# Opening of a two-layer cross-attention and FFN kernel: transposes, first scores and first maxima in another order

## What is computed

```python
def _L0_xattn_ref(Q, K, V, Wq, bq, Wk, bk, Wv, bv, Wo, bo):
    Qh = _split_heads(Q @ Wq.T + bq)
    Kh = _split_heads(K @ Wk.T + bk)
    Vh = _split_heads(V @ Wv.T + bv)
    scores = jnp.einsum('bhqd,bhkd->bhqk', Qh, Kh) / scale
    scores = scores - jnp.max(scores, axis=-1, keepdims=True)
    attn = jax.nn.softmax(scores, axis=-1)
    attn = jnp.clip(attn, EPS, None)
    attn = attn / jnp.sum(attn, axis=-1, keepdims=True)
    ctx = jnp.einsum('bhqk,bhkd->bhqd', attn, Vh)
    ...
def fp4_quant_dequant(x):
    xb = x.reshape(shape[:-1] + (shape[-1] // BLOCK, BLOCK))
    scale = jnp.max(jnp.abs(xb), axis=-1, keepdims=True) / 6.0
    ...
x = x + _L0_xattn_ref(_layernorm(x, axis=-1), ctx_1024, ctx_1024, ...)
x = x + _L0_ffn_ref(_layernorm(x, axis=-1), L0_ffn_w_gate, L0_ffn_w_up, L0_ffn_w_down)
x = x + _L1_xattn_ref(_layernorm(x, axis=-1), ctx_1024, ctx_1024, mask_BxSxS2_bk1, ...)
x = x + _L1_ffn_ref(_layernorm(x, axis=-1), L1_ffn_w1, L1_ffn_b1, L1_ffn_w2, L1_ffn_b2)
```

## Time and profile before

| | before |
|---|---|
| median of 3 runs | 927.75 us (927.74 to 927.95) |
| profiled execution, its own time | 927.82 us |
| its span, first to last instruction | 926.0 us |
| TensorE, VectorE, ScalarE, GpSimd busy | 97%, 72%, 65%, 22% of the span |
| granted TensorE clock | 1.000 |

### The profile page before, as it was taken

The page is one execution under the profiler, slowest core; times in us unless marked ns, Lnnn a source line. Parts: engine busy times, 40 slices in busy tenths (PEclk is TensorE's granted clock), DMA queues, the critical chain, the costliest instruction groups (busy, mean ns, idle before and its releaser), DMA issues.

```text
span 926.0 us, 16209 instructions
## 1 busy us (share of the span) xinstructions
PE 900.5 (97%) x5610; PEld 601.8 (65%) x5610; DVE 669.8 (72%) x2179; ACT 602.1 (65%) x1671; POOL 204.6 (22%) x316
## 2 busy tenths in 40 slices
PE   6899999999999999999999999999999999999998
PEld 3555576767665567576675566667757655757786
DVE  5999883763989786475598978367478988837568
ACT  3888425972789643795378953499257984269845
POOL 3211001862000000486000000077400000028600
PEclk9999999999999999999999999999999999999999
DMA  9500000000000000000000010000000000000000
GB/s 294 212 1 2 29 1 23 2 1 1 1 1 25 1 28 24 1 1 2 1 0 8 18 29 1 24 1 1 1 0 1 19 7 1 1 0 2 2 1 23
DMA packets 14560, 18.35 MB, mean 20 GB/s; under 512 B 3088, under 2 KB 11664, under 8 KB 14480
## 3 DMA queue, kind: packets, MB, share of 16 engines
q1 hardware_dynamic: 12288, 15.40, 5.0%
q10 hardware_dynamic: 2064, 1.91, 0.7%
q0 software_dynamic: 128, 0.01, 0.0%
HBM read 15.21 MB, written 2.10 MB: 19 GB/s over the span
## 4 chain that ended last, share of the span: by engine, by line
PE 76%; DVE 13%; ACT 8%; issue 3%; DMA 1%; SPq 0%; DVEq 0%; ACTq 0%
PE bank L1243 28%; PE bank L1258 10%; PE bank L1526 6%; PE bank L1624 6%; PE bank L1506 6%; PE bank L1358 5%; PE bank L1414 4%; ACT ring L671 4%; DVE row_max L1050 3%; PE bank L1391 3%; PE bank L1481 1%; PE bank L1492 1%; PE bank L1251 1%; PE bank L1430 1%; ACT ring L715 1%
## 5 line engine op out<-in xcount | busy, mean ns | idle before, releaser
L463 POOL TENSOR_TENSOR rstd<-var_eps,minus_half 128x2 f32<-128x2 f32 x32 | 23.3, 734 | 533.1 <-DVE var_eps L886 533.1
L481 POOL TENSOR_TENSOR ring<-ring,row_inv 128x256 f32<-128x256 f32 x192 | 112.1, 613 | 95.4 <-DVE row_inv L1145 95.4
L556 ACT ACTIVATE ring<-bank 128x512 f32<-128x512 f32 x224 | 123.6, 612 | 14.1 <-PE bank L1258 12.6
L1258 PE MATMUL bank<-ident_s,ring 128*128 128x128 f32 x768 | 105.0, 279 | 5.1 <-DVE ring L1058 2.7
L1258 PEld LDWEIGHTS bank<-ident_s,ring 128*128 128x128 f32 x768 | 82.8, 141 | 39.2 <-issue 15.7
L715 ACT ACTIVATE ring<-ring,row_max 128x256 f32<-128x256 f32 x192 | 95.1, 497 | 17.3 <-DVE row_max L1138 17.3
L671 ACT ACTIVATE ring<-bank,row_max 128x256 f32<-128x256 f32 x192 | 88.4, 496 | 5.7 <-DVE row_max L1050 5.7
L1138 DVE CUSTOM_DVE_ANT_0 ring<-bank,maskbias 128x256 f32<-128x256 f32 x192 | 70.7, 420 | 23.4 <-issue 23.4
L1050 DVE TENSOR_REDUCE row_max<-bank 128x2 f32<-128x512 f32 x128 | 79.4, 684 | 5.9 <-PE bank L1391 5.2
L1243 PE MATMUL bank<-wgu_s,act_s 128*128 128x352 f32 x256 | 78.4, 459 | 0.0
L1243 PE MATMUL bank<-ctxT_s,wk_s 128*128 128x512 f32 x160 | 76.4, 600 | 0.0
(11 more groups left out here) (192 smaller groups left out, 1753.3 us busy)
## 6 DMA issues: line engine op xcount, KB each, us to landing
x_s<-x SPq DMA_DIRECT2D x4, 512.0 KB, 3.9
ctxT_s<-ctxT SPq DMA_DIRECT2D x4, 512.0 KB, 4.2
w_s<-w SPq DMA_DIRECT2D x2, 1024.0 KB, 16.3
out<-act_s SPq DMA_DIRECT2D x16, 128.0 KB, 1.7
wk_s<-wk SPq DMA_DIRECT2D x1, 1024.0 KB, 13.4
wv_s<-wv SPq DMA_DIRECT2D x1, 1024.0 KB, 14.7
wq_s<-wq SPq DMA_DIRECT2D x1, 1024.0 KB, 16.2
wo_s<-wo SPq DMA_DIRECT2D x1, 1024.0 KB, 17.5
```

The lines of the kernel that those rows point to most:

```text
L481: ins = pool.tensor_tensor(probs1[i % PRING1][:, a, :], probs1[i % PRING1][:, a, :], row_inv[:, i, a:a + 1].to_broadcast([P, SEQ]), ALU.mult)
L556: act.activation(probsT[u % TRING][:, :, :].rearrange("p a q -> p (a q)"), psum(at, key)[:], ACT.Copy).then_inc(drain(at, key), 1)
L1258: ins = pe.transpose(psum(at, key)[:, c * SEQ + a * P:c * SEQ + (a + 1) * P], tile[:, a, c * P:(c + 1) * P], ident_s[:])
```

## The change

Five edits, all of the opening; nothing is computed differently.

- TensorE transposes `xn0` first, then makes key chunk 0, then the queries and the scores of round 0, and only then key chunk 1 and the values. The wait for the values' weights moves behind the scores.
- The banks of `xT0`, `k0` and `q0` follow: key chunk 1 goes to bank 7 instead of 1, the queries to banks 5 and 6 instead of 0 and 7.
- ScalarE takes out both halves of `xT0` and key chunk 0 ahead of `piece_steps(0)`; key chunk 1 is taken out between the second and the third unit's exponentials of round 0.
- VectorE takes the four maxima of round 0 ahead of `scale_piece(1)`, which now stands ahead of the values.

```diff
@@ jobs_layer0 @@
     for c in range(KEY_CHUNKS):
-        jobs.add(("k0", c), c)
+        jobs.add(("k0", c), c if with_last_layer else 7 * c)
...
     for c in range(KEY_CHUNKS):
-        jobs.add(("q0", c), c if with_last_layer else 7 * c)
+        jobs.add(("q0", c), c if with_last_layer else 5 + c)
@@ scalar: layer0_heads @@
                         for i in round_units0(r):
+                            if i == 2 and with_weights:
+                                layer0_keys(at, [1])
                             exponentials(i)
@@ scalar: opening @@
             act.wait_ge(keys_loaded, 16 * 4)
+            layer0_inputs(opening_pass)
+            layer0_keys(opening_pass, [0])
 
             piece_steps(0)
-            layer0_keys(opening_pass, [0])
-            layer0_inputs(opening_pass)
-            layer0_keys(opening_pass, [1])
             act.wait_ge(query_mask, 6)
@@ vector: layer0_heads @@
                         if g is None:
+                            scale_piece(1)
                             dve.wait_ge(values_loaded, 16 * 2)
@@ vector: opening @@
             round_piece(0)
-            scale_piece(1)
             dve.wait_ge(consts_set, 6)
@@ tensor: opening @@
-            pe.wait_ge(wk0_packed, 1)
-            pe.wait_ge(ctx_loaded, 16)
-            layer0_keys(opening_pass, [0])
             pe.wait_ge(ident_loaded, 16)
             for h in range(HALVES):
                 pe.wait_ge(xn_ready, 2 * h + 2)
                 transpose_xn(opening_pass, 0, h, xn0)
-            layer0_keys(opening_pass, [1])
+            pe.wait_ge(wk0_packed, 1)
+            pe.wait_ge(ctx_loaded, 16)
+            layer0_keys(opening_pass, [0])
             pe.wait_ge(wq0_packed, 1)
             layer0_queries(opening_pass)
+            layer0_scores(opening_pass, 0)
+            layer0_keys(opening_pass, [1])
             pe.wait_ge(values_loaded, 16 * 2)
-            layer0_scores(opening_pass, 0)
```

## The result

| | before | after |
|---|---|---|
| median (lowest to highest) | 927.77 us (927.38 to 928.12), 18 runs | 929.59 us (928.12 to 931.03), 18 runs |
| ratio, 95% interval | | 1.0017 (1.0011 to 1.0023) |
| profiled execution, its span | 927.82, 926.0 us | 928.34, 926.5 us |

The account below looks back on a forecast made before the run. On average TensorE bounds the kernel (97% busy), but the opening hangs on VectorE's first division: -0.53 us from the new order plus a 0.82 us stall gives +0.29, so 927.82 becomes 928.1 us, range 927.0 to 929.2.

Parts of the forecast that it names:

- TensorE's part: Opening on TensorE: queries start at 14.71 and scores at 18.41, both 2.86 us earlier; the 0.98 us wait goes.
- VectorE's part: VectorE's instructions up to the first division: the division comes at 25.92 against 26.45, -0.53 us before any stall.
- TensorE's 2.86 us: Earlier start of queries and scores; the rival that it comes through whole, 925.0, had 3%.
- The sum for the first division: VectorE's first reciprocal of a row sum: -0.53 us plus a stall of 0.82 gives +0.29 us.
- The stall is 0.82 us each time: VectorE's tensor_scalar in scale_piece(1), beside bias_x on GpSimd, is held up 0.82 us; this one-stall case had 42%.
- the first rival: In scale_piece(1), the stall lasts until bias_x ends, 1.57 us: +1.04 us at the first division, 928.9; 28%.
- three of the four meetings with `mask_to_bias`: Trace places where a VectorE TENSOR_SCALAR stalled beside GpSimd's mask_to_bias; three spoke against a stall until GpSimd ends.
- It decides only if the pause is long enough: Rival: TensorE's clock falls at its 2.7 us pause ahead of the first transposes, doubling 3.67 us; about 932; 4%.
- the clock's term: TensorE after its pause ahead of the first transposes: clock expected to stay at 1.00, nothing added.
- The range: Whole kernel: 927.0 to 929.2 us, the first three cases (927.3, 928.1, 928.9; 90%) with 0.3 at either end.
- my sum: GpSimd in the opening: bias_x follows directly on L492, starting at 22.21 and ending at 24.57.

Follow-up runs that it names:

- the repeated run: The changed kernel measured again with no edit: 929.60 us, ratio to before 1.0019; its profiled execution took 929.36 us at clock 0.998.
- the run with filling: Changed kernel plus two 128x512 matmuls, result not used, behind the values, so TensorE works through most of its pause: 928.11 us, ratio 1.0002.
- the last run: Kernel before with VectorE's edit alone, scale_piece(1) behind the maxima of round 0: 932.25 us, ratio 1.0048.
- the fastest kernel: Changed kernel with bias_x(0) ahead of L492 on its own load semaphore, two filling matmuls, and three warm-up matmuls instead of four: 926.39 us, ratio 0.9988.
- the kernel before with the longer pause: Kernel before plus one VectorE reduction over 768 columns, result unread, between the maxima of round 0 and the values: 928.63 us, ratio 1.0013.

## Why the prediction was wrong

- **"TensorE's part", "VectorE's part":** right. Where the warm-up ends near 12.1, scores, maxima and first division came within 0.1 us of the forecast, with the stall (26.72 against 26.74) and without it (25.87 against 25.92). That VectorE's full timeline swallows TensorE's 2.86 us was right: of these, 0.5 us reached the first division, and the stall took back more. The sum for the first division (+0.29) was right in the repeated run (+0.27).
- **"The stall is 0.82 us each time":** right in its place, and in its size (0.87 in one execution) only by chance. L837 ended at 24.00 and `bias_x` at 23.95; in the run with filling, 24.40 and 24.36. The stall lasts until GpSimd's instruction ends, which was the mechanism of the first rival; it came out short because `bias_x` began at 21.6 and not at 22.2. The Trainium skill's rule (SBUF — State Buffer, "Who interferes with whom") holds for this pair. What remains against it are three of the four meetings with `mask_to_bias`, of which nothing was tried.
- **"It decides only if the pause is long enough", 4%:** this step failed. The sum put the clock's term at nothing and had TensorE go through the pause "at clock 1.00". I had the pause at 2.7 us, one microsecond above the longest of the trace, and said that no row shows what the clock does then; the chance I gave it was that of a thing excluded. The pause came as forecast (2.75), and the clock fell. By their clock (0.998 or less) and their time (929.1 or more, the others 928.1 to 928.3) 25 of the 29 executions of the changed kernel had such a fall; one of them was traced. The price of the rival was mis-sized too: I had every instruction of round 1 at double time, 3.7 us; measured, an execution with a fall takes 1.3 to 1.4 us more (medians 929.6 and 928.3 of the first 18; 3.71 against 2.39 us up to the layer-1 keys). The lower level ends before those keys (1.98 us at 31.30 in the repeated run), and the transposes take 0.5 us more and not double. The 1.8 us are, as an estimate from the medians of the runs, about 0.3 from the first division (a gain of 0.5 to 0.6 less a stall of 0.9) and 1.5 from the clock, which the filling gave back.
- **A step that was missing:** TensorE's warm-up does not end at the same moment in each execution: between 11.8 and 13.4 us in the traces with four warm-up matmuls and this order, in which the clock rises at 9.8 to 13.0 us. Before, the 0.98 us of waiting ahead of the queries takes this in (with the warm-up's end at 12.63, in the last run, the queries still start at 17.41); after, nothing does. In the first profile this cost 1.1 us at the scores, and hid the stall besides.
- **The measurement:** I took one profile of before and its 0.2 us of spread for the width of the thing. The range allowed for one kind of execution; this kernel has two, with the fall and without.

## What to carry to other kernels

Work moved ahead leaves a pause behind it. Before moving TensorE's work forward to a point where another engine is the one that is late, write down how long TensorE will then stand still, and treat any pause longer than the trace has shown as a possible fall of its clock, with a chance that is not small; if useful work can't fill it, two matmuls for nothing may pay. And don't take one profile for the kernel: the first one here shows an execution without the fall, and the median is made of the others. Look, too, at who is released earlier by the move: a GpSimd instruction that was harmless beside reductions from PSUM stalled VectorE when it slid beside a tensor_scalar.

## What was not expected of the hardware

- One pause length, several outcomes: four kernels whose traces have 1.86 to 1.88 us of idle TensorE show 0.998 or less in 2, 4, 9 and 11 of 11 executions; in their traces the pause ends at 27.95, 27.86, 26.73 and 26.98. What exactly decides was not settled. The clock records of the five traces with a fall have one thing in common: the lower level begins 17.1 us after the rise in the warm-up (rises at 9.83 to 11.46 us, falls at 26.89 to 28.53), wherever the pause ends: 0.1 to 1.2 us before it in three of them, later in two. So the moment goes with the warm-up, which differs from one execution to the next, and not with the end of the pause. The Trainium skill says that an idle array is put back to its lower clock (TensorE: Matmul & The Clock Gate, Part 1); the traces agree that idleness does it, and show it at pauses under 2 us (1.87 and 1.88).
- The mean clock of an execution doesn't tell where the lower level lay: three executions of the fastest kernel show 0.998 and are no slower (926.3 to 926.4), and the kernel before has 15 of 87 at 0.998, only 0.4 us above the others (928.1 to 927.7). One place is the end: in the profile of the kernel before the lower level begins at 925.2, when TensorE has no more work, and lasts to the end of the span at 926.0. A 0.998 is a fall in the opening only where the time says so too.
- The lock works both ways. L492, eight columns on GpSimd, took 0.84 us in the kernel before, from 21.29, while VectorE was in L840 with two SBUF inputs, from 21.08 for 0.96 us; in the kernel before with the longer pause it took 0.73, beside the same instruction; in the changed kernel, beside a maximum from PSUM, 0.24. The Trainium skill has this side too (SBUF — State Buffer, "Who interferes with whom"): a VectorE instruction with two SBUF inputs contends with a GpSimd instruction that reads SBUF, and these rows agree. This is what moved `bias_x` by 0.6 us against my sum. No run was made for it.
